# Spreading a gated expert layer's coefficients with repeated DRAM reads instead of selector matmuls, and routing VectorE's first product through PSUM

## The chip, the cores and the metric

The kernel runs on one core of a Trainium2 chip. Its time is the device time in microseconds (us) of one execution. Of several runs the median counts.

## What is computed

The reference is a stack of four layers on x of shape 8 x 256 x 128 (2048 tokens of 128 numbers). Each layer adds a gated attention and then a gated feed-forward part to x. Only the feed-forward part of the second layer (layer 1, counted from 0) is touched:

```
x = x + tanh(g_ffn[1]) * L1_ffn(layernorm(x))

scores = sigmoid(x @ router_w.T)          # 64 experts; the 8 best, out of the 4 best groups, get a weight
coef   = (T, 64), zero but for the 8 chosen, which sum to 2.5
g = einsum('th,ehi->tei', x, Wg);  u = einsum('th,ehi->tei', x, Wu)      # i = 64 for each of the 64 experts
h = silu(g) * u * coef[:, :, None]
moe_out = einsum('tei,eih->th', h, Wd)
shared  = silu(x @ SWg) * (x @ SWu) @ SWd                               # 128 wide, no coefficient
out = moe_out + shared
```

So the coefficient of an expert and a token multiplies 64 hidden numbers, which lie on 64 partitions, and two experts fill the 128 partitions.

## The kernel before

The program is a sequence of stages: set-up, then for each layer attention, routing (`route_stage`) and experts (`expert_stage`; layer 0 has an `adapter_stage`). A stage is a block in which each engine runs its own list of instructions; between two stages all engines meet.

**Routing of layer 1.** VectorE works out the coefficients of all tokens, tokens on the partitions (`Bf`, 128 x 16 x 64, four bytes). It then splits them into a two-byte first part (L1094) and the rest (L1096) and signals `s_c`. TensorE turns the 16 tiles (L964), ScalarE copies the result to `coefT` (L996): 64 experts times two parts on the partitions, 2048 tokens along them.

**Experts.** `NC` = 4 chunks of `CH` = 512 tokens; in each, N = 33 blocks of 128 hidden numbers: block 0 is the shared expert, blocks 1 to 32 are two experts each. That makes 132 blocks. Weights, inputs and hidden numbers are carried as two-byte pairs, so each product takes three matmuls of 512 columns (`PRODUCTS`). Per block:

- TensorE (`do_up`, L1222): three matmuls for `u` into PSUM bank UB, three for `g` into GB (two banks each, used in turn). For blocks 1 to 32 then one selector matmul (L1235): a matrix of zeros and ones times `coefT` writes to bank CB the coefficient of each partition's expert for 512 tokens. It ends the block's signal `up`. A block waits until the one two before it has been weighed.
- ScalarE (L1290): silu of GB into `hid[..., 0, :]` in SBUF; then for the block before (L1298) the two-byte first part of the weighed numbers.
- VectorE (`weigh`): first product, activation times UB (L1334, written back to the same place in SBUF), a drain, second product, times CB (L1336, to `hid[..., 1, :]`). In block 0 there is one product only (L1331). It waits for `acted` (ScalarE) and `second` (GpSimd has read the place two blocks before).
- GpSimd (`split`, L1211): weighed numbers minus first part.
- TensorE (`do_down`, L1248): three matmuls that add the block three steps back to the output.

The order on each engine is written out by hand: `steps` emits the first five blocks of a chunk one by one and the other 28 as a hardware loop with four blocks a turn. In the loop the counts that waits compare with are worked out by register operations on the engine's queue. After a chunk ScalarE copies the output (L1304), TensorE turns it (L1257) and VectorE adds it to x (L1341).

SP, which issues DMAs, does nothing in these two stages. `Qs`, `Ks` (attention's operands in SBUF, four places each) and `xn` are idle there. Layers 2 and 3 use the same functions with `gated` false.

## Time and profile before

| | |
|---|---|
| Runs | 1461.1, 1466.1, 1471.67 us; median 1466.1 |
| Profiled execution | 1462.44 us |
| Its span, first to last instruction | 1460.7 us |
| Mean granted TensorE clock | 0.887 |
| TensorE busy (matmuls) | 1164.5 us, 80% |
| VectorE busy | 909.9 us, 62% |
| ScalarE busy | 782.0 us, 54% |
| GpSimd busy | 552.8 us, 38% |
| First to last selector matmul (L1235) | 402.0 to 682.9 us |

The shares are averages over stages with different limits. In the rows below, "idle before" is the time an engine stood still ahead of an instruction, and behind the arrow stands what ended it, as inferred from semaphore events. A wait for several things is put down to the last of them.
### The profile page before, as it was taken

The numbers are of one execution on the slowest core, as the hardware profiler recorded it, in microseconds if no ns is written. First come the engines' busy times: TensorE is split into PE (matmuls) and PEld (weight loads), VectorE is DVE, ScalarE is ACT, GpSimd is POOL, SyncE is SP. The second block draws the span as 40 slices with busy tenths as digits, with TensorE's granted clock in tenths as the row PEclk, the third lists the DMA queues.
The fourth block names the chain that finished last, engine by engine and source line by source line (L and its number), as shares of the span: only waits on it lengthen the run. The fifth ranks groups of instructions, "written<-read, shape, count | busy, mean of one in ns | idle before, by whom it ended". The sixth has DMA issues, their size and how long they took to land. (4 is left out here: it accounts for less than half of the span.)

```text
span 1460.7 us, 31201 instructions
## 1 busy us (share of the span) xinstructions
PE 1164.5 (80%) x10606; PEld 557.9 (38%) x10606; DVE 909.9 (62%) x1693; ACT 782.0 (54%) x1456; POOL 552.8 (38%) x604
## 2 busy tenths in 40 slices
PE   2678677886199999999667759999968866776997
PEld 1344354454144444444322323333434532233332
DVE  3668548784666666666879534444578757883443
ACT  1157412773155555554268537777637733783775
POOL 1105202551055555554225226777601201111775
PEclk9679967897599999999789959999969985997999
DMA  8721004100000000000611000000061013100001
GB/s 258 258 98 33 2 0 147 46 19 1 0 0 0 1 0 1 0 1 0 213 64 32 2 0 1 0 1 0 2 202 47 18 45 112 36 17 1 0 1 29
DMA packets 74898, 61.63 MB, mean 42 GB/s; under 512 B 12458, under 2 KB 72034, under 8 KB 73506
## 3 DMA queue, kind: packets, MB, share of 16 engines
q1 hardware_dynamic: 72498, 46.81, 10.5%
q10 hardware_dynamic: 2288, 13.31, 2.5%
q8 instruction: 73, 1.20, 0.3%
q14 instruction: 39, 0.32, 0.1%
HBM read 41.68 MB, written 18.09 MB: 41 GB/s over the span
## 5 line engine op out<-in xcount | busy, mean ns | idle before, releaser
L1211 POOL TENSOR_TENSOR work<-work 128x512 f16<-128x512 f32 x308 | 356.9, 1159 | 270.1 <-ACT work L1298 270.1
L726 ACT ACTIVATE work<-ps 128x384 f32<-128x384 f32 (+1 forms) x640 | 303.9, 533 | 185.0 <-PE ps L582 114.2
L823 DVE TENSOR_REDUCE bmax<-ps 128x6 f32<-128x768 f32 (+1 forms) x320 | 334.5, 1056 | 83.7 <-PE ps L560 56.5
L1222 PE MATMUL ps<-ao,wf 128*128 128x512 f16 x1320 | 343.2, 386 | 11.3 <-DVEq L1319 7.0
L1336 DVE TENSOR_TENSOR work<-work,ps 128x512 f32<-128x512 f32 x304 | 209.0, 688 | 174.8 <-POOL work L1211 131.5
L1248 PE MATMUL ps<-work,wf 128*128 128x512 f16 x924 | 252.1, 382 | 4.2 <-POOL work L1211 4.2
L1222 PEld LDWEIGHTS ps<-ao,wf 128*128 (+1 forms) x1320 | 123.4, 99 | 180.9 <-issue 44.4
L1298 ACT CAST work<-work 128x512 f16<-128x512 f32 x308 | 187.6, 609 | 3.3 <-DVE work L1336 1.5
L861 POOL TENSOR_SCALAR mx<-bmax 128x16 f16<-128x16 f32 x80 | 25.0, 313 | 382.9 <-DVE bmax L829 216.5
L571 PE MATMUL ps<-Qs,Ks 32*128 32x256 f16 x640 | 122.9, 293 | 56.9 <-DMA Qs<-mxT 23.6
L604 PE MATMUL ps<-work,V 128*9 128x256 f32 (+1 forms) x2560 | 157.6, 366 | 0.0
L1290 ACT ACTIVATE work<-ps,cols 128x512 f32<-128x512 f32 x176 | 120.8, 688 | 66.3 <-PE ps L1240 47.4
L1290 ACT ACTIVATE work<-ps 128x512 f32<-128x512 f32 x132 | 78.8, 597 | 135.3 <-DVE work L1336 125.4
L1334 DVE TENSOR_TENSOR work<-work,ps 128x512 f32<-128x512 f32 x128 | 88.1, 688 | 92.2 <-ACT work L1290 91.8
L1248 PEld LDWEIGHTS ps<-work,wf 128*128 (+1 forms) x924 | 81.9, 98 | 116.9 <-issue 36.8
L573 PE MATMUL ps<-Qs,Ks 32*128 32x128 f16 (+1 forms) x640 | 101.6, 251 | 15.5 <-ACT work L726 15.5
L553 PE MATMUL ps<-Ks,Qs 32*128 32x128 f16 (+1 forms) x640 | 87.6, 271 | 30.3 <-DMA Ks<-scrK 27.0
L555 PE MATMUL ps<-Ks,Qs 32*128 32x256 f16 x640 | 100.5, 313 | 0.0
L571 PEld LDWEIGHTS ps<-Qs,Ks 32*128 32x128 f16 x640 | 43.0, 92 | 140.2 <-issue 84.4
L339 POOL TENSOR_TENSOR rstd<-mom,neghalf 128x16 f32<-128x16 f32 x8 | 24.1, 3015 | 168.0 <-DVE mom L322 168.0
L604 PEld LDWEIGHTS ps<-work,V 128*9 128x9 f32 x2560 | 55.7, 92 | 64.2 <-issue 21.7
L582 PE MATMUL ps<-place,maskq 32*128 32x128 bf16 x640 | 64.9, 225 | 11.7 <-ACT work L726 11.7
(162 smaller groups left out, 1474.7 us busy)
## 6 DMA issues: line engine op xcount, KB each, us to landing
Qs<-scrQ SPq DMA_DIRECT2D x40, 256.0 KB, 3.2
Ks<-scrK SPq DMA_DIRECT2D x40, 256.0 KB, 3.4
scrK<-work SPq DMA_DIRECT2D x60, 128.0 KB, 2.1
scrQ<-work SPq DMA_DIRECT2D x60, 128.0 KB, 2.2
Qs<-mxT SPq DMA_DIRECT2D x320, 1.0 KB
wf<-in_L_w ACTq DMA_DIRECT2D x2, 1792.0 KB, 10.8
wf<-in_L_wg ACTq DMA_DIRECT2D x1, 2112.0 KB, 10.4
wf<-in_L_wu ACTq DMA_DIRECT2D x1, 2112.0 KB, 15.1
```

Source lines behind the costliest of these rows:

```text
L555: ins = pe.matmul(M[:, BW:BW + 256], q[:, 128:256], k[:, 0:256], start=False, stop=not causal)
L571: ins = pe.matmul(M[:, 0:256], k[:, 0:128], q[:, 0:256], start=True, stop=False)
L573: ins = pe.matmul(M[:, 256:W1], k[:, 128:256], q[:, 512 - W1:256], start=False, stop=not causal)
L604: ins = pe.matmul(ps[32 * j:32 * j + VW, OB, 256 * (k % 2) + first:256 * (k % 2) + 256], V[:, 2 * b + kt, 4 * at + j, :], prob[:, (4 * k + ...
L726: act.activation(prob[:, g % 8, 0:W1], ps[:, 4 + g % 3, 0:W1], ACT.Exp, scale=float(att["dk"]) ** -0.5).then_inc(exped, 1)
L823: dve.tensor_reduce(bmax[:, n // 4 % 2, 2 * (n % 4):2 * (n % 4) + 2, 0:NB], ps[:, b0:b0 + 2, 0:W1].rearrange("p i (n w) -> p i n w", n=NB) ...
L1211: pool.tensor_tensor(hparts[:, (m + r) % 4, 1, :], hid[:, (m + r) % 2, 1, :], hparts[:, (m + r) % 4, 0, :], ALU.subtract).then_inc(second, 1)
L1222: ins = pe.matmul(out, weight_parts(which, wpart, j), xh[:, xpart, c * CH:(c + 1) * CH], start=(i == 0), stop=(i == 2))
L1248: ins = pe.matmul(ps[:, YB + c % 2, :], weight_parts(m_["mats"] - 1, wpart, s), hparts[:, (m + r) % 4, hpart, :], start=(opens and i == 0) ...
L1290: act.activation(hid[:, (m + r) % 2, 0, :], ps[:, GB + (m + r) % 2, :], f, bias=bias).then_inc(acted, 1)
L1298: act.copy(hparts[:, (m + r - 1) % 4, 0, :], hid[:, (m + r - 1) % 2, 1, :]).then_inc(first, 1)
L1336: dve.tensor_tensor(h1, h0, coef, ALU.mult).then_inc(weighed, 1)
```

## The change

In layer 1's routing the split into two-byte parts, the two-byte transposes and the copy to `coefT` go. TensorE turns the four-byte coefficients (L978 of the changed kernel) into four PSUM banks, ScalarE copies each quarter to 64 partitions of `xn` as soon as it is there, and SP writes each quarter to a DRAM tensor `scrC` of 64 x 2048.

In layer 1's expert stage the selector matmul goes. For each block from 1 to 32 SP issues two DMAs: each reads the 512 coefficients (2 KB) of one expert 64 times, into 64 partitions of one of four places `cwide` (the memory of `Qs`). It waits until the block four before has been weighed. Each place has its own semaphore `coefs_in`, on which VectorE waits. VectorE's first product is written to the bank CB, now free, and the second takes it from there, multiplies it with `cwide` and writes to a ring of four places (the memory of `Ks`), from which ScalarE and GpSimd read. VectorE now waits for GpSimd's work four blocks before instead of two.

```diff
+        scrC = nc.dram_tensor("scrC", [64, T], F32, kind="Internal").ap()
+        crows = xn[0:64, :].rearrange("p (c k) -> p c k", c=NC)
+        cwide = Qs[:].rearrange("p b a t -> p (b a t)").bitcast(F32).rearrange("p (k c) -> p k c", k=4)
+        s_coef = sem("coefs_written")
+        weighted_ring = Ks[:].rearrange("p b a t -> p (b a t)").bitcast(F32).rearrange("p (k c) -> p k c", k=4)
...
@@ route_stage
+        @block.sync
+        def _(sp):
+            if l == 1:
+                for c in range(NC):
+                    sp.wait_ge(s_copied, c + 1)
+                    sp.dma_start(st["scrC"][:, c * CH:(c + 1) * CH], st["crows"][:, c, :]).then_inc(st["s_coef"], 16)
...
+            if l == 1:
+                for t in range(NT):
+                    ins = pe.transpose(ps[0:E, 2 + t // 4, t % 4 * P:(t % 4 + 1) * P], Bf[:, t, :], st["ident"][:])
+                    if t % 4 == 3:
+                        ins.then_inc(s_t, 1)
+                return
...
+            if l == 1:
+                for c in range(NC):
+                    act.wait_ge(s_t, c + 1)
+                    act.copy(st["crows"][:, c, :], ps[0:E, 2 + c, :]).then_inc(s_copied, 1)
+                return
...
+            if l == 1:
+                dve.sem_inc(s_c, 1)
+                return
...
@@ expert_stage
+        @block.sync
+        def _(sp):
+            if not gated:
+                return
+            sp.wait_ge(st["s_coef"], 16 * NC)
+            for c in range(NC):
+                for j in range(N - 1):
+                    if 32 * c + j >= 4:
+                        sp.wait_ge(weighed, 2 + N * c + j - 2 if j >= 4 else 2 + N * c - 3 + j)
+                    for half in range(2):
+                        sp.dma_start(cwide[64 * half:64 * half + 64, j % 4, :],
+                                     scrC[2 * j + half, c * CH:(c + 1) * CH].partition_broadcast(64)).then_inc(
+                                         coefs_in[j % 4], 16)
...
-                if gated and isinstance(s, int) and s == 0:
-                    pass
-                elif gated:
-                    ins = pe.matmul(ps[:, CB + (m + r) % 2, :],
-                                    sel[0:2 * E, bass.ds(s * P + (SEL_OFF[l] - P), P)],
-                                    coefT[0:2 * E, c * CH:(c + 1) * CH], start=True, stop=True)
-                elif r % 2 == 0:
+                if not gated and r % 2 == 0:
...
-                h0, h1 = hid[:, (m + r) % 2, 0, :], hid[:, (m + r) % 2, 1, :]
-                coef = ps[:, CB + (m + r) // per % 2, :]
+                h0, h1 = act_out(m + r), weighted(m + r)
+                coef = cwide[:, (r - 1) % 4, :] if gated else ps[:, CB + (m + r) // per % 2, :]
                 dve.wait_ge(acted, s + (m + 1))
-                dve.wait_ge(second, s + (m + 1))
+                if not gated:
+                    dve.wait_ge(second, s + (m + 1))
+                elif m + r >= 4:
+                    dve.wait_ge(second, s + (m - 1))
...
                 if gated:
-                    dve.tensor_tensor(h0, h0, ps[:, UB + (m + r) % 2, :], ALU.mult)
+                    dve.wait_ge(coefs_in[(r - 1) % 4], s * 8 + (32 * (8 * c + (r - 1) // 4 + 1) - 8 * r))
+                    dve.tensor_tensor(gated_out(m + r), h0, ps[:, UB + (m + r) % 2, :], ALU.mult)
                     dve.drain()
+                    h0 = gated_out(m + r)
                 dve.tensor_tensor(h1, h0, coef, ALU.mult).then_inc(weighed, 1)
```

`act_out(b)` is the place in `hid` that the activation had before, `gated_out(b)` is `ps[:, CB + b % 2, :]`, `weighted(b)` is the ring's place b % 4 when `gated`.

The order on two engines, in the hardware loop of layer 1's experts.
VectorE, before, two blocks:

```order
L1328 REGISTER_ALU
L1334 TENSOR_TENSOR work<-work,ps 128x512 [waits set_places_scaled,set_masks_loaded]
L1336 TENSOR_TENSOR work<-work,ps 128x512
L1328 REGISTER_ALU
L1334 TENSOR_TENSOR work<-work,ps 128x512 [waits set_places_scaled,set_masks_loaded]
L1336 TENSOR_TENSOR work<-work,ps 128x512
```

VectorE, now, the same two blocks:

```order
L1376 REGISTER_ALU
L1385 ISA [waits set_places_scaled,set_masks_loaded]
L1386 TENSOR_TENSOR ps<-work,ps 128x512 [waits r0_x_first]
L1389 TENSOR_TENSOR Ks<-ps,Qs 128x512
L1376 REGISTER_ALU
L1385 ISA [waits set_places_scaled,set_masks_loaded]
L1386 TENSOR_TENSOR ps<-work,ps 128x512 [waits r0_rows_copied]
L1389 TENSOR_TENSOR Ks<-ps,Qs 128x512
```

The waits for the activation and for GpSimd moved from the product to a register operation ahead of it, and the product itself waits for the coefficients.

TensorE, before, one block:

```order
L1222 ISA [waits set_ctx_loaded]
L1222 MATMUL ps<-ao,wf 128x512 x2
L1222 ISA
L1222 MATMUL ps<-ao,wf 128x512
L1222 ISA
L1222 MATMUL ps<-ao,wf 128x512 x2
L1222 ISA
L1222 MATMUL ps<-ao,wf 128x512
L1235 REGISTER_ALU
L1235 MATMUL ps<-coefT,sel 128x512
L1248 ISA [waits set_places_scaled]
L1248 MATMUL ps<-work,wf 128x512 x2
```

TensorE, now, one block:

```order
L1276 ISA [waits set_ctx_loaded]
L1276 MATMUL ps<-ao,wf 128x512 x2
L1276 ISA
L1276 MATMUL ps<-ao,wf 128x512
L1276 ISA
L1276 MATMUL ps<-ao,wf 128x512 x2
L1276 ISA
L1276 MATMUL ps<-ao,wf 128x512
L1296 ISA [waits set_places_scaled]
L1296 MATMUL ps<-work,wf 128x512 x2
```

The selector matmul and its register operation are gone; the six up matmuls and the down matmuls stand as they did, and a block starts with the wait for `weighed` on a register operation in both.

## Rows read from the trace of the kernel before

**Rows 1.** Window in layer 1's experts; PE, PEld, DVE, ACT, POOL, clock, DMA
```profile
500.00:550.00 50.00, 50.00 (x235) 22.97 (x234) 31.73 (x47) 25.54 (x48) 26.65 (x23) 1.00 0.00 0
```

**Rows 2.** Timeline, inner loop: start, length, engine, line, operation, [idle before, releaser]
```profile
499.82 1.46 PE L1222 MATMUL ps<-ao,wf 128*128 128x512 f16 x6
...
501.11 0.38 PE L1235 MATMUL ps<-coefT,sel 128*128 128x512 f16 x1
...
501.59 0.60 ACT L1290 ACTIVATE work<-ps 128x512 f32<-128x512 f32 x1 [1.05 <-DVE work L1336]
...
501.98 1.46 PE L1222 MATMUL ps<-ao,wf 128*128 128x512 f16 x6
...
502.22 0.69 DVE L1334 TENSOR_TENSOR work<-work,ps 128x512 f32<-128x512 f32 x1 [0.71 <-ACT work L1290]
...
502.98 0.69 DVE L1336 TENSOR_TENSOR work<-work,ps 128x512 f32<-128x512 f32 x1
```

**Rows 3.** Groups by line, 420 to 680 us; count, busy, mean ns, idle before
```profile
L1211 POOL TENSOR_TENSOR work<-work 128x512 f16<-128x512 f32 x120 | 139.0, 1158 | 120.3 <-ACT work L1298 120.3
...
L1290 ACT ACTIVATE work<-ps 128x512 f32<-128x512 f32 x121 | 72.3, 597 | 126.3 <-DVE work L1336 117.9 <-PE ps L1235 5.0 <-PE ps L1222 3.4
...
L1341 DVE SCALAR_TENSOR_TENSOR x<-ps,gate,x 128x512 f32<-128x512 f32 x2 | 1.5, 746 | 0.0
```

**Rows 4.** Timeline, a chunk's first block, which has no selector matmul
```profile
469.82 1.46 PE L1222 MATMUL ps<-ao,wf 128*128 128x512 f16 x6
...
471.37 0.60 ACT L1290 ACTIVATE work<-ps 128x512 f32<-128x512 f32 x1 [0.84 <-PE ps L1222]
```

**Rows 5.** All selector matmuls; count, ns min/median/max
```profile
L1235 PE MATMUL ps<-coefT,sel x128: 379/379/379, 402.0 to 682.9; 128*128 128x512 f16 x128
```

**Rows 6.** Timeline, the stage's first blocks
```profile
403.91 0.69 DVE L1336 TENSOR_TENSOR work<-work,ps 128x512 f32<-128x512 f32 x1
...
404.65 1.13 PEld L1222 LDWEIGHTS ps<-ao,wf 128*128 128x128 f16 x6 [0.17 <-DVE work L1336]
```

**Rows 7.** A register operation on VectorE's queue in the loop
```profile
L1198 DVEq FUSED_REGOPS  x64: 55/55/55, 410.5 to 1443.4; - x64
```

**Rows 8.** Timeline of routing: VectorE's add and multiply of one size
```profile
363.90 4.50 POOL L976 TENSOR_TENSOR ao<-xnT,ao 128x512 f16<-128x512 f32 x4 [6.61 <-ACT ao L987]
...
367.82 1.66 DVE L1008 TENSOR_TENSOR work<-work,rows 128x1024 f32<-128x1024 f32 x1 [6.30 <-ACT work L990]
...
379.27 1.23 DVE L1040 TENSOR_TENSOR work<-work,small 128x1024 f32<-128x1024 f32 x1
```

**Rows 9.** Timeline of SP's queue in the set-up: start, length of the issue
```profile
13.93 0.43 SPq L238 DMA_DIRECT2D rows<-in_rows  x1
```

**Rows 10.** Page, DMA issues; KB each, us to landing
```profile
Qs<-scrQ SPq DMA_DIRECT2D x40, 256.0 KB, 3.2
...
scrK<-work SPq DMA_DIRECT2D x60, 128.0 KB, 2.1
```

**Rows 11.** Windows of set-up and projections; last: DMA share, GB/s
```profile
20.00:22.00 2.00, 0.00 (x0) 0.00 (x0) 0.00 (x0) 0.00 (x0) 0.00 (x0) 1.00 1.00 405
36.00:38.00 2.00, 2.00 (x16) 1.65 (x15) 1.85 (x3) 1.88 (x4) 2.00 (x2) 1.00 0.25 97
```

**Rows 12.** Timeline: four-byte transposes and the end of layer 1's routing
```profile
358.49 0.72 PEld L348 LDWEIGHTS ps<-ident,xn 128*128 128x128 f32 x4 [10.76 <-DVE xn L331]
...
359.64 0.59 ACT L356 COPY xnT<-ps 128x512 f32<-128x512 f32 x1 [16.37 <-PE ps L348]
...
390.24 1.23 DVE L1091 TENSOR_TENSOR work<-work,small 128x1024 f32<-128x1024 f32 x1
...
393.59 1.89 PE L964 MATMUL ps<-identh,work 128*128 128x128 f16 x16 [26.96 <-DVE work L1096]
...
395.52 1.87 ACT L996 COPY coefT<-ps 128x2048 f16<-128x2048 f16 x1 [27.80 <-PE ps L964]
...
397.82 0.58 PE L1222 MATMUL ps<-ao,wf 128*128 128x512 f16 x1 [2.35 <-DVEq L1319]
```

More of the change, by code:

```diff
@@ L945, in route_stage @@
     s_xh = sem(f"r{l}_x_first")
+    s_copied = sem(f"r{l}_rows_copied")
     def wide(v, e=E):
@@ L1186, in expert_stage @@
     GB, UB, CB, YB = 0, 2, 4, 6
+    cwide, scrC = st["cwide"], st["scrC"]
+    ring = st["weighted_ring"] if gated else None
+    coefs_in = [sem(f"e{l}_coefs_in{k}") for k in range(4)] if gated else None
     g = st["gate"][:, 4 + l:5 + l]
@@ L1189, in expert_stage, with act_out, gated_out, weighted @@
     PRODUCTS = ((0, 0), (0, 1), (1, 0))
+    def act_out(b):
+        return hid[:, b % 2, 0, :]
+    def gated_out(b):
+        return ps[:, CB + b % 2, :]
+    def weighted(b):
+        return ring[:, b % 4, :] if gated else hid[:, b % 2, 1, :]
     def weight_parts(which, part, j):
@@ L1210, in split @@
                 pool.wait_ge(first, s + (m + 1))
-                pool.tensor_tensor(hparts[:, (m + r) % 4, 1, :], hid[:, (m + r) % 2, 1, :],
+                pool.tensor_tensor(hparts[:, (m + r) % 4, 1, :], weighted(m + r),
                                    hparts[:, (m + r) % 4, 0, :], ALU.subtract).then_inc(second, 1)
@@ L1289, in activate @@
                 bias = 0.0 if l < 2 else cols[:, bass.ds(s + C_OFF["b1", l], 1)]
-                act.activation(hid[:, (m + r) % 2, 0, :], ps[:, GB + (m + r) % 2, :], f,
+                act.activation(act_out(m + r), ps[:, GB + (m + r) % 2, :], f,
                                bias=bias).then_inc(acted, 1)
@@ L1297, in first_part @@
                 act.wait_ge(weighed, s + (m + 2))
-                act.copy(hparts[:, (m + r - 1) % 4, 0, :], hid[:, (m + r - 1) % 2, 1, :]).then_inc(first, 1)
+                act.copy(hparts[:, (m + r - 1) % 4, 0, :], weighted(m + r - 1)).then_inc(first, 1)
             def copy_output(c):
```

## The prediction

> **What bounds the kernel now.** The change touches layer 1's routing and its expert stage, so I read one window of that stage first, then a timeline of single blocks, then the groups by line. In the window the reader is to see TensorE busy for all of 50.00 us at granted clock 1.00 (the 2.4 GHz level), with VectorE at 31.73, ScalarE at 25.54, GpSimd at 26.65 and almost no DMA [rows 1]. "Busy" alone proves little for pipelined matmuls, so the timeline has to say it: block after block starts at 499.82 and 501.98, 2.16 us apart, and holds ten matmuls of 512 columns (six up, one selector, three down), so one takes 0.216 us and no gap is left [rows 2]. The stage has 132 such blocks.
>
> The groups by line seem to contradict this: ScalarE's activation idles 126.3 us, of which 117.9 are put down to VectorE's L1336 [rows 3]. The timeline shows why that is a coincidence. The activation of 501.59 starts 0.10 us after the selector matmul of 501.11 has ended (501.49), and VectorE's previous product happened to end nearby. In a chunk's first block, which has no selector, ScalarE starts at 471.37 for a block begun at 469.82, 1.55 us after it instead of 1.77, and its releaser is now TensorE [rows 2, 4]. So TensorE's stream sets the pace, and ScalarE waits for the block's last matmul.
>
> **The selector matmuls go.** There are 128, from 402.0 to 682.9 us [rows 5]. On an engine without a gap each is worth its 0.216 us: 128 x 0.216 = 27.6 us. Blocks 1 to 3 of the stage are not paced by TensorE: there a weight load waits for VectorE's product (403.91 + 0.69 = 404.60, load at 404.65) [rows 6], so about half of those three shows: minus 0.3. That leaves 27.3 us, if TensorE stays the bound at 9 x 0.216 = 1.944 us a block.
>
> **What is late next.** The up matmuls of block b+2 overwrite the PSUM banks of block b and wait for VectorE to have weighed b. From the start of b: ScalarE starts at 1.55 [rows 4], VectorE 0.63 later (501.59 to 502.22), its second product 0.76 after the first, and that lasts 0.69: 3.63 us [rows 2]. The wait is passed 0.05 us later [rows 6], and in the loop a register operation of TensorE's queue carries it, for which I add 0.05 (an estimate from 55 ns on VectorE's queue [rows 7]): 3.73. Two blocks take TensorE 3.888. The margin is 0.16 us per two blocks, and the change spends part of it. In the order of VectorE's loop the waits for "activated" and "second part" now hang on a register operation (it computes the coefficient count) that stands between them and the product; before, they hung on the product itself. That is one operation of 0.055 us [rows 7] behind the wait, two in one block of four: 3.79 to 3.84. Still under 3.888, by 0.05 to 0.10.
>
> The first product now writes PSUM and the second reads it there. No row of before shows VectorE writing PSUM. From below I take 0: VectorE's products lasted 0.69 with one operand in PSUM [rows 2], and while TensorE is the bound a faster product gains nothing. From above, the slowest 512-column VectorE operation with a PSUM source is L1341 with 746 ns, 0.06 more [rows 3]; for both products 0.12, which would overrun the margin by 0.02 to 0.07 per two blocks, 1 to 5 us over 132 blocks. I take the product's own 0.69 as the nearest row and put 1 us aside for blocks in which the margin is used up.
>
> The PSUM detour has its reason in a row: an add of 1024 columns with both sources in SBUF took 1.66 us where it began beside a GpSimd operation that ran until 368.40, while a multiply of that size, alone, took 1.23 [rows 8]. With the coefficients in SBUF, a second product out of SBUF would meet GpSimd's 1.16 us split in every block [rows 3]. Each product keeps one operand in PSUM, so I expect none of this. The ring of four only lets VectorE run further ahead of GpSimd, whose 1.16 us is well under 1.944; it is worth nothing and costs nothing by itself. The relaxed wait for "second part" had been met anyway: VectorE's idle time ahead of the first product is put down to ScalarE [rows 2].
>
> **The coefficients by DMA.** Each block needs two transfers of 128 KB, each reading one 2 KB row 64 times. An issue costs SP 0.43 us [rows 9], two a block 0.9 of 1.944, and SP has nothing else to do here. The pair for block r is released when block r-4 has been weighed, and is wanted when r reaches VectorE: 4 x 1.944 - 1.45 (the two products, 0.76 + 0.69) = 6.3 us later. A transfer of 128 KB lands 2.1 us after its issue, one of 256 KB after 3.2 [rows 10]. So the pair is there 0.9 + 3.2 = 4.1 us after its release at the latest, 2.2 us early. The rate needed is 262 KB per 1.944 us = 135 GB/s. In the set-up, while the 128-fold broadcasts of a row and of the mask were in the queue, the engines moved 405 GB/s [rows 11]. Cost in the middle of the stage: 0, hidden behind four blocks.
>
> **The routing's end.** Before: 6.35 us pass from the end of L1091 (390.24 + 1.23 = 391.47) to the first expert matmul at 397.82: two VectorE operations until 393.59, 16 two-byte transposes (1.89), a copy of 1.87, and the stage change of 0.43 behind its end [rows 12]. Now: no VectorE operation; 16 four-byte transposes, of which four took from 358.49 to the copy at 359.64 [rows 12], so 16 take about 3.8 (0.226 each from the last one's start, at the same low clock); ScalarE copies each quarter behind them, only the last shows, 0.59; then SP issues that quarter's write, 0.43, and the stage change follows, 0.43: about 5.3 us. Gain 1.0. The write lands 2.1 us after its issue, SP then issues the first pair (0.9), which lands 2.1 to 3.2 later: 5.1 to 6.2 us after the last issue began. Block 1's first product stood at 403.91 - 0.75 = 403.16, 5.34 us after the first matmul [rows 6, 12], which is 6.2 us after that issue began (0.43 + 0.43 + 5.34). So it is met, in the worst case just.
>
> **Sum.** 27.3 + 1.0 - 1.0 = 27.3 us. The profiled execution took 1462.44 us (span 1460.7, 1.7 around it): 1435.1. It lies 3.7 us under the median 1466.1 of the runs shown, so against that median the forecast is 1438.8, say 1439.
>
> **Rivals.** (1) The loop over ScalarE and VectorE becomes the bound. For it: the margin left is under a tenth of a microsecond. If the PSUM write, the drain behind it and the queue operations together put 0.3 us on the chain, two blocks take 3.73 + 0.30 = 4.03, a block 2.015, 0.071 over TensorE: 132 x 0.071 = 9.4 us, 1448. Against it: no row asks for more than 0.23 (0.11 of queue operations, 0.12 of products).
>
> (2) The repeated reads can't keep up. All engines fetch the same 2 KB at once, which no row of before shows for rows that short; the set-up's repeated rows were 6 and 8 KB. The point from which this decides is 2.158 us a pair, 121 GB/s: below, the kernel is slower than before. As a price I take the lowest rate of a window full of 128 KB transfers, 97 GB/s [rows 11], though that window was paced by SP: 262 KB then take 2.70 us, 0.54 more than now, 128 x 0.54 = 69 us, about 1534. Against it stand the 405 GB/s.
> The Trainium skill has a rule that points this way: its page "DMA: Bandwidth & Descriptors", section "Latency and other measured facts", reports copies whose rows lie a large power of two apart in DRAM falling from 207 to 103 GB/s, and infers that parallel streams then meet in one memory channel. 64 reads of one row would be the extreme of that; at 103 GB/s the sum would be 2.54 us a block, some 50 us more than before. No row here shows such a fall.
>
> (3) The start costs more than it gains: coefficients late for block 1, and a stalled TensorE that stays at its lower clock for longer. 3.2 us late at most (a whole 256 KB landing again), with two blocks of nine matmuls at the 1.2 GHz level, twice the 0.216 each, another 3.9: 1439 + 3.2 + 3.9 = 1446. It stays on the faster side.
>
> **How the numbers follow.** TensorE paces all but the start (my forecast, rival 3 in its upper part): 0.66. Rival 1: 0.18. Rival 2: 0.12 for slower than before, and 0.04 for a pair time between 2.1 and 2.2 us, which gives about no change. Range: the low end is 1466.1 - 28.6 (nothing set aside), less 4 for the spread of the runs: 1433. The high end takes in rival 1 and the same spread: 1453. Outside stay rival 2 and its neighbour. About 1% (some 15 us) is what a measurement of this kernel can tell from no change. Faster by more: the forecast and nearly all of rival 1, 0.83; within: 0.05; slower: 0.12.
>
> **What would show it.** In the profile after: 128 matmuls fewer; blocks 1.94 to 1.95 us apart at clock 1.00; ScalarE's activation 1.55 us behind a block's first matmul; both products at 0.69. TensorE gaps ahead of a block released by VectorE mean rival 1; VectorE's first product released by a DMA in the middle of the stage, with a pair landing over 6.3 us after its release, means rival 2; the same only in the first blocks means rival 3. A second product over 0.75 us would mean that GpSimd is in the way after all. The forecast is wrong if block starts lie more than 2.0 us apart.

## The result and the profile after

The changed kernel takes 1442.0 us (median of four runs, 1440.1 to 1450.4) against 1468.9 for the kernel before in the same comparison (four runs, 1461.1 to 1474.2): a ratio of 0.984, with an interval of 0.980 to 0.988. That is faster by 1.2 to 2.0%, or by 17 to 29 us. The forecast was 1439, with a range of 1433 to 1453. The profiled execution took 1440.67 us.

Totals mix stages which the change doesn't touch, so I first cut the span where the stages meet. The kernel before, the first instruction of the stage behind layer 1's experts (it began those at 397.82 [rows 12]):

```profile
690.75 0.49 DVE L311 BATCH_NORM_STATS2 stats<-x 128x6 f32<-128x128 f32 x2 [0.32 <-PEq L1202]
```

The changed kernel, timeline of the routing's end and the stage's start, then the next stage's first instruction:

```profile
385.52 1.23 DVE L1116 TENSOR_TENSOR work<-work,small 128x1024 f32<-128x1024 f32 x1
...
386.83 3.62 PE L978 MATMUL ps<-ident,work 128*64 128x128 f32 x16 [24.46 <-DVEq L1117]
...
388.53 3.01 SPq L963 DMA_DIRECT2D scrC<-xn  x4
...
390.49 0.58 ACT L1017 COPY xn<-ps 64x512 f32<-64x512 f32 x1 [0.28 <-PE ps L978]
...
392.38 4.25 PE L1276 MATMUL ps<-ao,wf 128*128 128x512 f16 x12 [1.93 <-DVEq L1367]
...
393.31 4.94 SPq L1253 DMA_DIRECT2D Qs<-scrC  x8
...
397.71 0.69 DVE L1386 TENSOR_TENSOR ps<-work,ps 128x512 f32<-128x512 f32 x1
...
665.15 1.06 DVE L317 BATCH_NORM_STATS2 stats<-x 128x6 f32<-128x128 f32 x5 [0.32 <-PEq L1242]
```

So layer 1's experts took 690.75 - 397.82 = 292.9 us before and 665.15 - 392.38 = 272.8 after: 20.2 us less. The tail of the routing, from the end of the last large multiply (L1091 before, L1116 now) to the first expert matmul, took 6.35 us [rows 12] and now takes 392.38 - 386.75 = 5.63: 0.7 less. That is the change: 20.9 us of the 21.8 between the two profiled executions. Everything else is the same work, with differences of both signs: the program up to layer 1's routing is identical and came out 7.0 us shorter in this execution, the routing ahead of its tail 2.3 us longer, and what follows the stage 3.8 longer. I therefore read most experiments below by the length of the experts' stage ("the stage"), from its first matmul to the next stage's first instruction.

Window 500 to 550 us of the changed kernel; columns as in [rows 1]:

```profile
500.00:550.00 50.00, 50.00 (x231) 20.97 (x229) 34.73 (x51) 28.10 (x51) 29.05 (x26) 1.00 0.41 127
```

TensorE again shows 50.00 of 50 at clock 1.00, and 127 GB/s of DMA are new. "Busy" is full in both, yet TensorE is no longer always the bound. The timeline shows it:

```profile
500.35 0.60 ACT L1338 ACTIVATE work<-ps 128x512 f32<-128x512 f32 x1 [0.84 <-PE ps L1276]
500.63 3.03 SPq L1253 DMA_DIRECT2D Qs<-scrC  x4
...
500.78 1.47 PE L1276 MATMUL ps<-ao,wf 128*128 128x512 f16 x6
...
501.09 0.69 DVE L1386 TENSOR_TENSOR ps<-work,ps 128x512 f32<-128x512 f32 x1 [0.48 <-ACT work L1338]
...
501.86 0.69 DVE L1389 TENSOR_TENSOR Ks<-ps,Qs 128x512 f32<-128x512 f32 x1
...
502.34 0.60 ACT L1338 ACTIVATE work<-ps 128x512 f32<-128x512 f32 x1 [0.89 <-PE ps L1276]
...
503.17 0.70 DVE L1386 TENSOR_TENSOR ps<-work,ps 128x512 f32<-128x512 f32 x1 [0.62 <-ACT work L1338]
...
504.29 0.60 ACT L1338 ACTIVATE work<-ps 128x512 f32<-128x512 f32 x1 [0.84 <-PE ps L1276]
...
505.11 0.70 DVE L1386 TENSOR_TENSOR ps<-work,ps 128x512 f32<-128x512 f32 x1 [0.48 <-ACT work L1338]
```

VectorE starts 0.74 us after the activation (500.35 to 501.09), where it was 0.63 before [rows 2], and 0.83 and 0.82 in the next two blocks (502.34 to 503.17, 504.29 to 505.11). The two products lie 0.77 apart and last 0.69 to 0.70. Read over the whole stage, the distance is 0.63 to 0.64 outside the hardware loops, but for the stage's first product (0.74). In the loops it is 0.72 to 0.74, but 0.82 to 0.83 (0.86 once) in one block of four in the first chunk and in two of four in the others. In the last chunk a third of the four lies at 0.84 to 0.86 (1.11 the first time):

```profile
624.60 0.60 ACT L1338 ACTIVATE work<-ps 128x512 f32<-128x512 f32 x1 [0.98 <-PE ps L1276]
...
625.45 0.69 DVE L1386 TENSOR_TENSOR ps<-work,ps 128x512 f32<-128x512 f32 x1 [0.73 <-ACT work L1338]
```

In the first chunk's loop one sees what a block waits for:

```profile
405.47 1.46 PE L1276 MATMUL ps<-ao,wf 128*128 128x512 f16 x6
...
406.72 0.69 DVE L1389 TENSOR_TENSOR Ks<-ps,Qs 128x512 f32<-128x512 f32 x1
...
407.57 0.33 PEld L1276 LDWEIGHTS ps<-ao,wf 128*128 x3 [0.49 <-issue]
407.58 0.60 PE L1276 MATMUL ps<-ao,wf 128*128 128x512 f16 x2
...
415.54 0.82 PE L1276 MATMUL ps<-ao,wf 128*128 128x512 f16 x3
```

The product ends at 407.41 and TensorE's next block starts with the load at 407.57, 0.16 later. This block began 2.11 us behind the one before it, and its weight load, though marked "issue", came right behind VectorE's product. Four blocks take 415.54 - 407.58 = 7.96 us, 1.99 each instead of 1.944. By chunk, four blocks of the loop take 7.95, 7.97, 7.97 and 8.07 us on average.

The groups from 430 to 640 us and the page's DMA issues answer to [rows 3, 10]:

```profile
L1265 POOL TENSOR_TENSOR work<-Ks,work 128x512 f16<-128x512 f32 x106 | 122.9, 1160 | 88.7 <-ACT work L1346 88.7
L1386 DVE TENSOR_TENSOR ps<-work,ps 128x512 f32<-128x512 f32 x103 | 71.7, 696 | 57.0 <-ACT work L1338 57.0
L1389 DVE TENSOR_TENSOR Ks<-ps,Qs 128x512 f32<-128x512 f32 x102 | 70.6, 692 | 7.6
L1338 ACT ACTIVATE work<-ps 128x512 f32<-128x512 f32 x105 | 62.8, 598 | 92.1 <-PE ps L1276 91.0 <-DVE Ks L1389 1.1
```

```profile
Qs<-scrC SPq DMA_DIRECT2D x256, 128.0 KB, 3.0
```

No product waits for a DMA. The coefficients land 3.0 us after their issue and are never late.

### The profile page after: what moved, and what is told of

It is laid out like the page before. It is cut to its first block and busy times, and to the rows that moved or that the text cites. A ratio compares the mean times of both kernels' runs of the same rounds, so it can differ in the third digit from the quotient of the medians.

```text
span 1438.8 us, 31204 instructions
## 1 busy us (share of the span) xinstructions
PE 1137.6 (79%) x10478; PEld 535.6 (37%) x10478; DVE 909.3 (63%) x1691; ACT 782.5 (54%) x1459; POOL 552.9 (38%) x604
## 5 line engine op out<-in xcount | busy, mean ns | idle before, releaser
L1265 POOL TENSOR_TENSOR work<-work 128x512 f16<-128x512 f32 x176 | 203.9, 1159 | 108.1 <-ACT work L1346 108.1
L1389 DVE TENSOR_TENSOR work<-work,ps 128x512 f32<-128x512 f32 x176 | 120.9, 688 | 166.7 <-POOL work L1265 133.8
L1265 POOL TENSOR_TENSOR work<-Ks,work 128x512 f16<-128x512 f32 x132 | 153.1, 1160 | 146.7 <-ACT work L1346 146.7
L1276 PEld LDWEIGHTS ps<-ao,wf 128*128 (+1 forms) x1320 | 115.8, 99 | 195.0 <-issue 84.6
L610 PE MATMUL ps<-work,V 128*9 128x256 f32 (+1 forms) x2560 | 153.8, 359 | 0.0
L1386 DVE TENSOR_TENSOR ps<-work,ps 128x512 f32<-128x512 f32 x128 | 89.1, 696 | 70.3 <-ACT work L1338 70.3
L1346 ACT CAST work<-work 128x512 f16<-128x512 f32 x176 | 107.0, 608 | 1.9 <-PE ps L1296 1.4
L1389 DVE TENSOR_TENSOR Ks<-ps,Qs 128x512 f32<-128x512 f32 x128 | 88.6, 692 | 9.6
```

The source lines that it names most:

```text
L610: ins = pe.matmul(ps[32 * j:32 * j + VW, OB, 256 * (k % 2) + first:256 * (k % 2) + 256], V[:, 2 * b + kt, 4 * at + j, :], prob[:, (4 * k + ...
L1265: pool.tensor_tensor(hparts[:, (m + r) % 4, 1, :], weighted(m + r), hparts[:, (m + r) % 4, 0, :], ALU.subtract).then_inc(second, 1)
L1276: ins = pe.matmul(out, weight_parts(which, wpart, j), xh[:, xpart, c * CH:(c + 1) * CH], start=(i == 0), stop=(i == 2))
L1346: act.copy(hparts[:, (m + r - 1) % 4, 0, :], weighted(m + r - 1)).then_inc(first, 1)
L1389: dve.tensor_tensor(h1, h0, coef, ALU.mult).then_inc(weighed, 1)
```

## The experiments

All are the changed kernel with one edit. "Product" is VectorE's. The kernel before took 1457.0 to 1473.8 us beside them.

| | total, us | stage, us |
|---|---|---|
| before | 1462.44 (profiled) | 292.9 |
| the change | 1440.67 (profiled) | 272.8 |
| e1 coefficients awaited first | 1439.1 (median of 6) | 266.3 |
| e2 few bytes | 1445.5 | 271.6 |
| e3 first product back in SBUF | 1493.8 | 315.2 |
| e4 ring of two | 1453.3 | 268.9 |
| e5 tenth matmul | 1460.2 | 294.2 |
| e6 a third transfer, same row | 1614.9 | 437.7 |
| e7 two places | 1506.2 | 338.2 |
| e8 third, 128 rows of the weights | 1463.8 | 289.9 |
| e9 third, one row of the weights | 1476.1 | 296.6 |
| e10 pair not repeated | 1437.0 | 273.2 |
| e11 third, another coefficient row | 1581.2 | 407.2 |
| e12 third, 128 pieces of the coefficients | 1471.2 | 294.1 |

**What puts a block at 1.99 us: register operations or traffic?**

```diff
# e1_coefs_first
-                dve.wait_ge(acted, s + (m + 1))
+                if gated and not (isinstance(s, int) and s == 0):
+                    dve.wait_ge(coefs_in[(r - 1) % 4], s * 8 + (32 * (8 * c + (r - 1) // 4 + 1) - 8 * r))
...
+                    dve.wait_ge(acted, s + (m + 1))
...
-                    dve.wait_ge(coefs_in[(r - 1) % 4], s * 8 + (32 * (8 * c + (r - 1) // 4 + 1) - 8 * r))
                     dve.tensor_tensor(gated_out(m + r), h0, ps[:, UB + (m + r) % 2, :], ALU.mult)
```

> The changed kernel, but VectorE waits for the coefficients and for the second part first and for the activation last, so that the register operations that work out the counts run while VectorE is idle anyway, and the product itself carries the wait for the activation. Register theory: in the changed kernel VectorE's first product starts 0.74 us (three blocks of four) or 0.86 us (the fourth) after ScalarE's activation starts instead of 0.63; that makes the loop over ScalarE and VectorE 3.90 to 4.06 us for two blocks against TensorE's 3.89, and four blocks take 7.96 us instead of 7.78. Here the product starts 0.63 us after the activation in all blocks, four blocks take 7.78 us, TensorE's starts are even, and the kernel is 5 to 6 us faster than the changed one, 1435 us beside 1441. Traffic theory (transfers into SBUF slow a matmul, a weight load or a product): no change in the four-block time of 7.96 us. PSUM theory (the product by way of PSUM is what is late): no change either, within 1 us.

The waits are the same, in another order: coefficients, "second part", "activated". Only the last is late, and no register operation stands behind it any more. Window and timeline of e1:

```profile
500.00:550.00 50.00, 50.00 (x235) 22.29 (x234) 35.18 (x51) 29.02 (x53) 29.18 (x26) 1.00 0.45 130
```

```profile
501.75 0.60 ACT L1338 ACTIVATE work<-ps 128x512 f32<-128x512 f32 x1 [0.84 <-PE ps L1276]
...
502.38 0.70 DVE L1389 TENSOR_TENSOR ps<-work,ps 128x512 f32<-128x512 f32 x1 [0.48 <-ACT work L1338]
...
503.15 0.69 DVE L1392 TENSOR_TENSOR Ks<-ps,Qs 128x512 f32<-128x512 f32 x1
...
503.69 0.60 ACT L1338 ACTIVATE work<-ps 128x512 f32<-128x512 f32 x1 [0.84 <-PE ps L1276]
```

The product starts 0.63 us after the activation in every block of the loops, activations are 1.94 apart, and the stage is 6.5 us shorter than the change's. TensorE is as "busy" as in the change but did 235 matmuls in these 50 us instead of 231. The distances of 0.82 to 0.86 are gone as well, in all four chunks, and four blocks take 7.77. The stage's ends in e1:

```profile
391.48 1.86 PE L1276 MATMUL ps<-ao,wf 128*128 128x512 f16 x4 [1.93 <-DVEq L1367]
...
657.75 0.49 DVE L317 BATCH_NORM_STATS2 stats<-x 128x6 f32<-128x128 f32 x2 [0.32 <-PEq L1242]
```

The ratio to the kernel before is 0.982 (0.979 to 0.985); the totals alone wouldn't tell it from the change (0.984), the stages do.

```diff
# e2_few_bytes
+                        w = CH if c == 0 and j < 4 else 8
...
-                                     scrC[2 * j + half, c * CH:(c + 1) * CH].partition_broadcast(64)).then_inc(
+                                     scrC[2 * j + half, c * CH:c * CH + w].partition_broadcast(64)).then_inc(
```

> The changed kernel with the same 256 transfers and the same waits, but after the first four pairs each moves 8 of the 512 coefficients, so the products of later blocks use left-over coefficients. Traffic theory: four blocks go from 7.96 us back toward 7.78 us, VectorE's products from 0.696 and 0.692 to 0.688 us, and a pair lands in about 2.1 us instead of 3.0. Register theory and PSUM theory: four blocks stay at 7.96 us, kernel within 1.5 us of the changed one but for its spread.

After the first four pairs only 8 of 512 columns are read, and the products use what the places already hold. The window of e2 from 420 to 620 us shows 2 GB/s. The pattern stays: 7.96 us for four blocks, products of 0.696 and 0.692, a stage of 271.6. The DMA traffic into SBUF isn't what slows VectorE or the loop.

```diff
# e4_ring_two
     def weighted(b):
-        return ring[:, b % 4, :] if gated else hid[:, b % 2, 1, :]
+        return hid[:, b % 2, 1, :]
...
-                if not gated:
-                    dve.wait_ge(second, s + (m + 1))
-                elif m + r >= 4:
-                    dve.wait_ge(second, s + (m - 1))
+                dve.wait_ge(second, s + (m + 1))
```

> The changed kernel without the ring of four: the weighed numbers go to the two old places in SBUF and VectorE waits for GpSimd's work of two blocks before instead of four. My theory: GpSimd has been done for over 0.5 us when VectorE asks, so a block stays at 1.99 us and the kernel within 1 us plus spread. Rival (the ring carries part of the gain): VectorE's first product is released by GpSimd in a part of the blocks, a block takes over 2.02 us.

I had taken the ring as costing nothing. It costs about 4 us: without it the stage is 268.9, 3.9 shorter than the change's. With the ring "second part" is compared with another count than "activated"; with two places both waits compare with the same count and one register operation is enough. Timeline of e4:

```profile
550.76 0.60 ACT L1338 ACTIVATE work<-ps 128x512 f32<-128x512 f32 x1 [0.89 <-PE ps L1276]
...
551.49 0.70 DVE L1383 TENSOR_TENSOR ps<-work,ps 128x512 f32<-128x512 f32 x1 [0.53 <-ACT work L1338]
```

The distance is 0.72 to 0.75 in the loops; the 0.82 to 0.86 are gone, but for one block. Four blocks take 7.87. The one register operation that is left still costs 268.9 - 266.3 = 2.6 us against e1. (The total of e4, 1453.3, is high because this execution came to layer 1's routing 12 us later than the change's, through the same program, and took 4.6 us more behind the stage.)

**Is it the matmul that was removed?**

```diff
# e5_tenth_matmul
                 if gated:
+                    if not (isinstance(s, int) and s == 0):
+                        pe.matmul(ps[:, UB + (m + r) % 2, :], weight_parts(1, 0, s), xh[:, 0, c * CH:(c + 1) * CH],
+                                  start=True, stop=True)
                     product(ps[:, UB + (m + r) % 2, :], 1, s, c)
```

> The changed kernel with one more matmul of 512 columns in each of the blocks 1 to 32 of a chunk (the first one for u runs twice, with the same result), in the selector's place on TensorE. TensorE theory: blocks are again 2.16 us apart, no gap is left on TensorE, and the stage from its first matmul to the next stage's first VectorE operation takes 292 us as before the change (292.9), against 272.8 in the changed kernel. So the transfers, the PSUM detour and the ring are worth nothing in themselves, and the gain is the matmuls alone. Rival (the loop over ScalarE and VectorE, 0.10 to 0.23 us longer now, binds here too): blocks of 2.2 us and more, a stage of 297 us or more, slower than before.

A tenth matmul of 512 columns opens each of these blocks (the selector closed its group; either way seven matmuls end before the activation starts), and nothing else goes back. The six up matmuls start at 501.06 and 503.22, 2.16 us apart. The stage's ends:

```profile
391.65 1.86 PE L1276 MATMUL ps<-ao,wf 128*128 128x512 f16 x4 [1.93 <-DVEq L1370]
...
685.87 3.19 DVE L317 BATCH_NORM_STATS2 stats<-x 128x6 f32<-128x128 f32 x16 [0.32 <-PEq L1242]
```

It takes 294.2 us, 1.3 more than before the change, and the kernel 1460.2, against 1459.2 for the kernel before beside it. The stage's gain is the 128 matmuls; DMA, detour and ring bring nothing of their own.

**What the detour through PSUM is worth.**

```diff
# e3_product_in_sbuf
     def gated_out(b):
-        return ps[:, CB + b % 2, :]
+        return act_out(b)
```

> The changed kernel with the first product written back to SBUF in place of the free PSUM bank, so the second product has both sources in SBUF. Port theory (two SBUF sources on VectorE meet GpSimd's split of 1.16 us in each block): the second product grows from 0.69 us to 0.9 to 1.2 us on average, the loop for two blocks from 3.96 to 4.2 to 4.5 us, a block takes 2.1 to 2.25 us, and the stage is 15 to 35 us longer, which gives back half of the gain or all of it. Rival: the detour does nothing, the second product stays at 0.69 to 0.70 us and a block at 1.99 us; the gap between the two products shrinks from 0.77 to 0.76 us if the PSUM write costs anything.

Groups of e3 from 430 us on, and its timeline:

```profile
L1389 DVE TENSOR_TENSOR Ks<-work,Qs 128x512 f32<-128x512 f32 x89 | 92.3, 1037 | 6.6
```

```profile
500.00 1.15 POOL L1265 TENSOR_TENSOR work<-Ks,work 128x512 f16<-128x512 f32 x1 [0.54 <-ACT work L1346]
...
500.32 1.39 DVE L1389 TENSOR_TENSOR Ks<-work,Qs 128x512 f32<-128x512 f32 x1
...
502.38 0.69 DVE L1389 TENSOR_TENSOR Ks<-work,Qs 128x512 f32<-128x512 f32 x1
502.43 1.65 POOL L1265 TENSOR_TENSOR work<-Ks,work 128x512 f16<-128x512 f32 x1 [1.28 <-ACT work L1346]
```

The second product now has both sources in SBUF. Where GpSimd was already running (500.00), the product takes 1.39 us instead of 0.69; where the product came first (502.38), GpSimd's split takes 1.65 instead of 1.16. Two blocks take 4.62 us, the stage 315.2, 42 us more than with the detour and more than the 15 to 35 expected: this version is slower than the kernel before. The Trainium skill, page "SBUF — State Buffer", section "SBUF: two separate sides", says that a VectorE operation with two SBUF inputs and a GpSimd operation that reads SBUF hold one port pair for a whole instruction, and that the second of them waits. By that rule the product would have ended at 501.15 + 0.69 = 501.84 and the split at 503.07 + 1.16 = 504.23; they ended at 501.71 and 504.08. The trace agrees to within 0.15 us, here and in all 128 blocks of the stage: the product came second in 77 and the split in 51, and each ended 0.13 to 0.15 us before that sum.

**How close are the coefficient reads to being the bound?**

```diff
# e7_two_places
-                    if 32 * c + j >= 4:
-                        sp.wait_ge(weighed, 2 + N * c + j - 2 if j >= 4 else 2 + N * c - 3 + j)
+                    if 32 * c + j >= 2:
+                        sp.wait_ge(weighed, 2 + N * c + j if j >= 2 else 2 + N * c - 1 + j)
...
-                        sp.dma_start(cwide[64 * half:64 * half + 64, j % 4, :],
+                        sp.dma_start(cwide[64 * half:64 * half + 64, j % 2, :],
...
```

> The changed kernel with two places for the coefficients instead of four: a pair is released when the block two before has been weighed. Cover theory: a pair needs 0.59 for the first issue and then about 0.6 plus 3.0 us for the second to land, 4.2 us, and then the two products, 1.46: 5.6 us for two blocks, 2.8 us a block, stage 370 us, kernel 1540 us; with four places 4 x 1.99 - 1.46 = 6.5 us were there for the 4.2. Rival (a pair lands in under 2.5 us once fewer are in flight): 3.97 us for two blocks still hold it and a block stays near 2.0 us.

Two blocks take about 5.1 us and the stage 338.2, not the 370 expected; the product idles for the DMA (group from 420 to 620 us):

```profile
L1386 DVE TENSOR_TENSOR ps<-work,ps 128x512 f32<-128x512 f32 x78 | 54.3, 696 | 84.6 <-DMA Qs<-scrC 80.9 <-ACT work L1338 3.7
```

With half the lead the reads set the pace. Two blocks then are the two products (1.46) and the time from a pair's release to its landing: 5.1 - 1.46 = 3.6 us, under the 4.1 that I had allowed. With four places 6.3 us are available.

The next five add a third transfer of 256 KB (2 KB into each of 128 partitions of `xn`) to each pair, so the bytes double. VectorE's wait asks for it too; its data is not used. They differ in what it reads; the line of e6 stands for all:

```diff
# e6_twice_the_bytes
+                    sp.dma_start(xn[:].rearrange("p (k c) -> p k c", k=4)[:, j % 4, :],
+                                 scrC[2 * j, c * CH:(c + 1) * CH].partition_broadcast(P)).then_inc(
+                                     coefs_in[j % 4], 16)
...
# e8_straight_third reads
+                                 st["dr"]["L1_wg"][:, CH * (j % 8):CH * (j % 8 + 1)]).then_inc(
# e9_third_elsewhere reads
+                                 st["dr"]["L1_wg"][j:j + 1, CH * (j % 8):CH * (j % 8 + 1)].rearrange("o c -> (o c)").partition_broadcast(P)).then_inc(
# e11_third_other_row reads
+                                 scrC[(2 * j + 32) % 64, c * CH:(c + 1) * CH].partition_broadcast(P)).then_inc(
# e12_third_straight_same reads
+                                 scrC.rearrange("r (h k) -> (r h) k", h=2)[:, CH * (j % 2):CH * (j % 2 + 1)]).then_inc(
```

> The changed kernel with a third transfer for each block, which reads one row 128 times (256 KB) into idle memory and is waited for as the other two are. 524 KB a block is 263 GB/s at 1.99 us a block. Cover theory: the engines moved 405 GB/s in the set-up, SP's three issues take 3 x 0.59 = 1.8 us, under a block's time, and the three land in under 6.3 us: the block stays at 1.99 us, the stage at 272.8 us, within 1 us. Hot-row theory (repeated reads of 2 KB meet in one place in DRAM): the rate stays near the changed kernel's 130 to 150 GB/s, a block takes 3.5 to 4 us and the kernel over 1600 us. Issue theory: SP's three issues take longer than a block; then a block takes what they take, 2.0 to 2.5 us.

> As the kernel with twice the bytes, but the third transfer of a block (256 KB, into idle memory) reads 128 different rows of 2 KB of a weight tensor in DRAM instead of one row 128 times. With the repeated row a block took 3.2 us, the engines moved 158 GB/s at a DMA share of 0.89 and a transfer landed after 7.4 to 8.5 us. Hot-row theory (reads of one 2 KB row come out of one place in DRAM that gives about 150 GB/s or less): the third transfer no longer competes there, a block takes 2.0 to 2.2 us and the engines move 240 GB/s or more. Size theory (2 KB pieces into SBUF, or SP's three issues, are the limit whatever is read): a block still takes 3.0 us or more at about 160 GB/s.

> As before, but the third transfer reads one row 128 times that lies in another DRAM tensor (a weight tensor, another row in each block). Hot-row theory, the place is a row's own: each of the streams may have its own place, so a block is faster than 3.2 us, but each 128-fold read (256 KB) at 150 GB/s still takes 1.7 us; block 2.0 to 2.8 us. If the limit is on repeated reads as such, wherever the row lies: again 3.0 to 3.3 us and 158 GB/s. Size theory: the same 3.0 us or more as for different rows.

> As the kernel with twice the bytes, but the third transfer reads 128 times a row of the same DRAM tensor that neither of the block's two other transfers reads (32 rows on, 256 KB away). With the row of the first transfer the engines moved 158 GB/s and a block took 3.2 us; with a row of another tensor 233 GB/s and about 2.2 us. Row theory (one row gives about 120 GB/s: 192 reads of 2 KB in 3.2 us): a block takes 2.1 to 2.3 us at 225 to 240 GB/s as with the other tensor. Region theory (rows of the small coefficients' tensor share one place): 3.0 us or more and 160 GB/s again.

> As the kernel with twice the bytes, but the third transfer reads 128 different pieces of 2 KB, 4 KB apart, of the coefficients' own DRAM tensor. So far: third transfer one row of this tensor 128 times 158 and 169 GB/s, of a weight tensor 233 GB/s, different rows of a weight tensor 238 GB/s. Repetition theory (the same few KB read again and again within one tensor are slow): 230 GB/s or more, a block 2.0 to 2.3 us. Place theory (the 512 KB tensor as a whole lies where reads are slower): 160 to 180 GB/s and a block of 2.9 to 3.3 us here too.

Windows from 420 to 620 us; the last two columns are the share of the DMA engines and GB/s. The change, e6, e11, e12, e8 and e9, in this order:

```profile
420.00:620.00 200.00, 199.79 (x912) 83.19 (x911) 138.49 (x200) 112.17 (x204) 116.34 (x101) 1.00 0.42 128
```

```profile
420.00:620.00 200.00, 128.57 (x553) 49.18 (x551) 83.98 (x122) 73.67 (x123) 70.20 (x61) 1.00 0.87 159
```

```profile
420.00:620.00 200.00, 146.05 (x616) 56.84 (x616) 92.06 (x133) 81.40 (x139) 78.79 (x68) 0.97 0.94 170
```

```profile
420.00:620.00 200.00, 191.61 (x850) 77.06 (x849) 128.88 (x187) 106.98 (x189) 108.43 (x94) 1.00 1.02 238
```

```profile
420.00:620.00 200.00, 191.83 (x856) 77.88 (x854) 129.69 (x188) 106.99 (x190) 109.03 (x94) 1.00 1.01 241
```

```profile
420.00:620.00 200.00, 188.54 (x834) 75.53 (x833) 126.22 (x182) 104.95 (x185) 106.36 (x92) 1.00 0.99 235
```

With a third, repeated read of the pair's own row the core moves 159 GB/s, a block takes 3.3 us and the kernel is 156 us slower than the one before beside it. With another coefficient row (e11) it is 170 GB/s. With 128 different pieces of the same tensor (e12) it is 238, with 128 rows of the weights (e8) 241, with one weight row 128 times (e9) 235. So neither the bytes nor the number of transfers makes e6 slow, nor is it the one row: reading few short rows of the coefficient tensor many times is capped at 159 to 170 GB/s, well below what half repeated, half different reads reach. In e8, e9 and e12 the DMA engines' share is 0.99 to 1.02, so there the engines themselves are full, and the product waits for the third transfer: the stage is 17 to 24 us longer than the change's. In e6 they move a third less at a share of 0.87. DMA issues on the pages of e6 and e12:

```profile
Qs<-scrC SPq DMA_DIRECT2D x256, 128.0 KB, 7.4
xn<-scrC SPq DMA_DIRECT2D x128, 256.0 KB, 8.5
```

```profile
xn<-scrC SPq DMA_DIRECT2D x128, 256.0 KB, 5.9
Qs<-scrC SPq DMA_DIRECT2D x256, 128.0 KB, 4.9
```

Does the repetition cost anything at the change's own rate?

```diff
# e10_straight_pair
-                                     scrC[2 * j + half, c * CH:(c + 1) * CH].partition_broadcast(64)).then_inc(
+                                     scrC[:, c * CH:(c + 1) * CH]).then_inc(
```

> The changed kernel with its two transfers a block, but each reads 64 different rows of 2 KB of the coefficients' DRAM tensor instead of one row 64 times, so every product takes wrong coefficients. Hot-row theory: a transfer lands 2.1 to 2.3 us after its issue instead of 3.0, at a lower DMA share than 0.41 for the same 127 to 131 GB/s; SP's issue falls from 0.59 toward 0.43 us; the block stays at 1.99 us since VectorE's chain sets it. Size theory: 3.0 us and 0.41 again.

Each transfer now reads 64 different rows (and the products use other coefficients). The stage takes 273.2 us against 272.8, at the same share of 0.42 and 128 GB/s, and a landing 2.9 against 3.0; the 2.1 to 2.3 that the hot-row theory asked for didn't come. At 128 GB/s repetition costs nothing.

## Why the prediction was right, and which term was mis-sized

**The source of the gain: right. The bound: only in part.** The 128 selector matmuls were the gain: e5 puts one a block back and the gain is gone. In e1, where nothing else is late, the stage is 292.9 - 266.3 = 26.6 us shorter, against 27.3 by the sum. But the forecast's "TensorE paces all but the start" doesn't hold in the hardware loops of the change. There TensorE waits for VectorE in every turn, which is rival 1's mechanism. By the prediction's own sign, block starts more than 2.0 us apart, one block start in four is late (2.08), while the mean is 1.99 in the first three chunks and 2.02 in the last.

**What is late next: the right loop, but its length too small.** This is the mis-sized term: 1 us was set aside for blocks in which the margin is used up, and 27.3 - 20.2 = 7.1 us were missing from the stage. e1 gives back 6.5 of them; the other 0.7 isn't explained. The forecast's loop was 3.79 to 3.84 us for two blocks. The trace after gives 1.55 + 0.74 + 0.77 + 0.69 + 0.17 = 3.92, and 4.01 to 4.04 where the product starts 0.83 to 0.86 behind; the two together come within 0.04 us of the 7.96 of four blocks. TensorE needs 4 x 1.944 = 7.78 for them. A block is released by the one two before it, so two such chains run side by side: a second late block in the other chain costs nothing (7.95 in the first chunk, 7.97 in the next two), one in the same chain does (8.07 in the last). Over seven turns a chunk, against the 7.77 of e1, that is 7 x (0.18 + 0.20 + 0.20 + 0.30) = 6.2 us. Two steps of the working made it too short:

- "One operation of 0.055 us behind the wait, two in one block of four." The count was right in the first chunk alone; in the others it is two blocks of four. The size was wrong: one costs 0.11 (0.63 to 0.74), two 0.20 to 0.23. [Rows 7] show how long one register operation lasts, not the time it puts between a wait and what follows. e1 removes both from behind the wait, with 6.5 us; e4 removes the second, with 3.9. The third block of the last chunk's turns has one such operation only, and the product starts later behind it; why is open, but the delay goes with either edit.
- The release of TensorE: 0.05 in straight code [rows 6] plus 0.05 for the register operation. It is 0.16 to 0.18 in the loop, 0.11 more than in straight code, presumably by the same error; no run tests it apart.

The bounds of this cost were drawn from the duration of one row, and the upper bound of the products was spent where nothing was lost. Rival 1 described this mechanism with 0.30 us more on the 3.73 of two blocks, 9.4 us for the stage. On average 0.25 came (7.97 / 2 - 3.73), and 7.1 us, so the truth lies between forecast and rival, and nearer the rival. At its chance of 0.18 it was rated too low.

**The PSUM product: right.** 0.696 and 0.692 us against 0.688, and a distance of 0.77 against 0.76. The low end of its bounds was the true one. The reason given for the detour is shown by e3: 42 us without it.

**The ring "costs nothing": wrong,** about 4 us (e4), part of the same term. Its wait compares with another count, which needs a register operation of its own behind the late wait, in one block of four of the first chunk and two of four later. Freed of GpSimd's distance of two, VectorE gained nothing: it had not been waiting for GpSimd.

**The coefficients hidden behind four blocks: right,** but with less to spare than the working suggested. The rate of 405 GB/s in [rows 11] was the only evidence for repeated reads, and its repeated rows were three and four times as long. Short repeated rows stop at 159 to 170 GB/s (e6, e11); the change needs 262 KB per 1.99 us, 132 GB/s. Rival 2 didn't come, and its mechanism exists: the point from which it decides was put at 121 GB/s. The rule that the prediction takes from the Trainium skill ("DMA: Bandwidth & Descriptors", "Latency and other measured facts") is on rows a large power of two apart, not on one row read again and again. The fall here was to 159, not to its 103 GB/s, and whether streams meet in one memory channel, as the page infers, isn't settled by these runs.

**The routing's tail: 0.7 instead of 1.0.** Transposes, the last copy and its write took 3.66, 0.58 and 0.47 us, close to 3.8, 0.59 and 0.43. The stage change behind the issue took 392.38 - 391.54 = 0.84 instead of 0.43. **Rival 3 (a costly start): not seen.** Block 1's product starts at 397.71, 5.33 us behind the first matmul; before it was 5.34.

**The totals.** The medians differ by 26.9 us, which looks like the 27.3 of the sum. That is luck: what the change did is 20.9, by the profiled executions, and the ratio of 0.984 means 23. The rest is the spread of stages that the change leaves alone. The forecast was right on the range and on where the gain comes from; 6.4 of its 27.3 us didn't come.

## What to carry to other kernels

In a hardware loop, put waits whose counts need register operations ahead of the wait that is met last; one operation behind the late wait cost 0.11 us a block here, twice its own duration. When two engines' loops lie within a few per cent of each other, compare starts of blocks and the length of the stage, since "busy" stays full and totals spread by more than the effect. Where VectorE works beside GpSimd, keep one operand of each VectorE operation in PSUM, even by a detour.

## What the runs showed of the hardware

- Repeated reads of a few short DRAM rows of one tensor have a ceiling of their own: 159 GB/s for three reads over two rows of 2 KB a block, 170 with a third row. As soon as half of the bytes came from different pieces or from another tensor it was 235 to 241, and the DMA engines were full. Why a repeated row of the weights (e9) doesn't count towards it, and what exactly is shared, stays open.
- At that ceiling SP's issues stretch as well: the median of one rose from 0.59 us in the change to 1.04 in e6, and the landing from 3.0 to 7.4.
- The first product's place in PSUM costs next to nothing (0.696 us against 0.688), but both sources in SBUF beside GpSimd cost up to 0.95 us on VectorE (1.64 instead of 0.69, in e3's last chunk) or 0.50 on GpSimd, whichever came second. The routing shows it once more: an add that took 1.66 beside GpSimd [rows 8] took 1.23 in the changed kernel's execution, where GpSimd had finished.
